# One Mamba-2 layer with MLP and experts: the scan's quadratic part on two halves of 64 tokens instead of one block of 128

## The reference, cut to what matters

```python
dt = softplus(zxbcdt[..., -N_HEADS:] + dt_bias)
decay = exp(dt * -exp(A_log))
def step(h, t):                       # h: (B, 24, 16, 64), one step per token
    dec, dtt, xt, bt, ct = t
    h = dec[..., None, None] * h + (dtt[..., None] * xt)[..., None] * bt[:, None, None, :]
    y = einsum('bhpn,bn->bhp', h, ct)
    return h, y
y = (ys + D * xh) * silu(z)
```

## Time and profile before

| | |
|---|---|
| profiled execution, its own time | 1016.41 us |
| its span | 1014.4 us, mean granted clock 0.962 |
| PE, share of the span | 81% |
| PE weight loads | 63% |
| DVE | 65% |
| ACT | 58% |
| POOL | 34% |

### The profile page before, as it was taken

One profiled execution on the slowest core, in us unless ns is written; L12 is line 12 of the kernel. 1 busy time (PEld: TensorE's weight loads), 2 busy tenths in 40 slices (PEclk: granted clock), 3 DMA queues, 4 the chain that ended last, 5 costly groups with the idle time before them and its releaser, 6 DMA issues.

```text
span 1014.4 us, 22717 instructions
## 1 busy us (share of the span) xinstructions
PE 825.3 (81%) x7120; PEld 637.8 (63%) x7120; DVE 660.8 (65%) x1629; ACT 585.1 (58%) x1307; POOL 345.4 (34%) x508
## 2 busy tenths in 40 slices
PE   3363898888888888888888888888888888888867
PEld 2232676666667666666767666666766666676656
DVE  5565675757667685766768575766768576665524
ACT  3574565665656666665656566565666666565423
POOL 1222333343324344333433334332434433242402
PEclk9675999999999999999999999999999999999988
DMA  8200000000000000000000000000000000000000
GB/s 221 81 1 12 2 6 15 2 20 0 19 0 5 14 0 19 0 19 0 5 14 4 15 0 19 0 20 0 5 14 0 19 0 19 0 5 9 1 8 8
DMA packets 16466, 15.22 MB, mean 15 GB/s; under 512 B 6322, under 2 KB 15224, under 8 KB 16184
## 3 DMA queue, kind: packets, MB, share of 16 engines
q1 hardware_dynamic: 16440, 14.89, 5.5%
HBM read 10.69 MB, written 4.19 MB: 15 GB/s over the span
## 4 chain that ended last, share of the span: by engine, by line
PE 42%; DVE 23%; issue 16%; ACT 13%; POOL 3%; DVEq 1%; ACTq 1%; DMA 0%; POOLq 0%; SPq 0%
PE bank L1305 20%; DVE mr L1024 5%; DVE xa L966 4%; PE bank L1471 4%; PE bank L1513 3%; PE bank L1588 3%; PE bank L1537 3%; DVE w_raw L1188 2%; ACT L687 2%; ACT xk L651 2%; ACT L812 2%; ACT er L706 2%; DVE e_ge L1117 2%; POOL t L476 1%; PE bank L1450 1%
## 5 line engine op out<-in xcount | busy, mean ns | idle before, releaser
L1024 DVE SCALAR_TENSOR_TENSOR mr<-er,gm 128x512 f32<-128x512 f32 x192 | 129.2, 702 | 58.1 <-ACT er L706 57.7
L540 POOL TENSOR_TENSOR w_raw<-w_raw 128x384 f32<-128x384 f32 x96 | 99.2, 1034 | 145.9 <-ACT w_raw L767 143.6
L778 ACT ACTIVATE sg<-bank 128x256 f32<-128x256 f32 x144 | 55.3, 384 | 136.2 <-PE bank L1305 135.9
L1588 PE MATMUL bank<-w2t,w_raw 128*128 128x192 f32 x576 | 116.4, 329 | 7.4 <-ACT w_raw L767 7.4
L706 ACT ACTIVATE er<-bank 128x512 f32<-128x512 f32 x192 | 104.3, 597 | 30.4 <-PE bank L1450 29.9
L1471 PE MATMUL bank<-mr,xd 128*32 128x128 f32 x1536 | 90.9, 288 | 28.0 <-DVE mr L1024 26.6
L966 DVE SCALAR_TENSOR_TENSOR xa<-xr,cw_,xa 128x256 f32<-128x256 f32 x192 | 101.4, 536 | 4.4 <-ACT xa L617 0.4
L1305 PE MATMUL bank<-x_h,w_hi 128*128 128x256 f16 x288 | 79.9, 277 | 29.6 <-DVE w_raw L1188 27.5
L1188 DVE TENSOR_TENSOR w_raw<-sg,bank 128x256 f32<-128x256 f32 x144 | 60.3, 420 | 61.5 <-ACT sg L778 56.3
L1588 PEld LDWEIGHTS bank<-w2t,w_raw 128*128 128x128 f32 x576 | 90.5, 190 | 13.3 <-ACT w_raw L767 9.6
L737 ACT ACTIVATE sg<-bank 128x256 f32<-128x256 f32 x96 | 36.9, 384 | 105.2 <-PE bank L1305 104.8
(11 more groups left out here) (233 smaller groups left out, 2160.4 us busy)
## 6 DMA issues: line engine op xcount, KB each, us to landing
out<-w_raw SPq DMA_DIRECT2D x16, 192.0 KB, 2.0
w_raw<-weights SPq DMA_DIRECT2D x1, 1924.0 KB, 9.6
wt_raw<-weights SPq DMA_DIRECT2D x2, 962.0 KB, 14.9
pos<-position SPq DMA_DIRECT2D x16, 96.0 KB, 2.8
tok<-tokens SPq DMA_DIRECT2D x16, 70.0 KB
sums<-lj SPq DMA_DIRECT2D x16, 64.0 KB, 2.2
ri<-sums SPq DMA_DIRECT2D x64, 12.0 KB
w2t<-w SPq DMA_DIRECT2D x1, 864.0 KB, 19.7
```

Source lines behind the costliest of these rows:

```text
L540: pool.tensor_tensor(acc[:], acc[:], wt_out[:, e % NWT], ALU.add).then_inc(acc_done, 1)
L778: act.activation(sg[:, e % 2, :], p_pair[e % 2][:, 0:NB * Q], ACT.Silu).then_inc(sx_ready, 1)
L1024: ve.scalar_tensor_tensor(mr[:, r % NER], er[:, r % NER], 1.0, gm[:, b, :].unsqueeze(1).to_broadcast([128, HG, Q]), ALU.min, ALU.mult)\
L1588: ins = pe.matmul(p_out[(e + 1) % 2][:, b * D:(b + 1) * D], hh[:, e % NHH, b * Q:(b + 1) * Q], w2t[:, e, :], start=True, stop=True)
```

## The change

A chunk's 128 tokens are taken as two halves of 64 (`QB`). Pairs of tokens within one half go through the exponent, mask and product path; partition j of a tile holds the first half's j in 0..63 and the second half's in 64..127, so one tile of 128 x 512 now covers 8 heads (`HG` = 8, `NQ` = 3, 6 units a chunk). `exponents` for the middle unit of a sequence is two matmuls of 256 columns. The products are done for each half by itself: 64 rows, 64 columns, by `masked_products`; the second group on the same unit waits for the first (`yh_done`).

What the second half takes from the first goes through a middle state: POOL makes `middle` = `state` times the decay over the first half and `xm` = `xd` times the decay from j to the middle (`to_middle`, ahead of `weighted_x` in each scan), and `state_read` becomes nine fp32 matmuls of 64 columns: `state` for the first half, `middle` and `xm` (with `gx`, the C·B products of the second half with the first) for the second. It waits for both POOL results. `ends` doubles to four sets, by six more matmuls in `running_sums`. `masked_g` becomes three operations.

`ri` has 64 instead of 128 columns a head, and is filled by 16 DMAs of two partitions, each row in pieces of 64 fp16 values, instead of 4. `setup_first` on VectorE has nine operations more (masks `ones_first`, `after_first`, zeros), `setup_exponents` half as wide ones.

Orders change too: on TensorE `state_share(f, 0)` and `project_in_x(p)` move ahead of the last products of their scan; on VectorE the state read's scaling (`from_state`), `mixed` and `pre_onehot`, and `norm2_apply` and `steps_dt` come behind the last mask of their scan; on ScalarE `mixed_norm` comes behind the third exponential.

```diff
-HG = 4
+HG = 8
+QB = Q // 2
...
+def unit_parts(q):
+    parts = []
+    for f in range(2):
+        heads = range(max(q * HG, f * HF), min((q + 1) * HG, (f + 1) * HF))
+        if len(heads):
+            parts.append((f, heads[0] - f * HF, heads[0] - q * HG, len(heads)))
+    return parts
...
-        ends = sb("ends", [128, 2, NB, NH])
-        eend, wend = ends[:, 0], ends[:, 1]
+        ends = sb("ends", [128, 4, NB, NH])
+        eend, wend, emid, wmid = (ends[:, k] for k in range(4))
...
-        ri = sb("ri", [128, NB, 2, HF, Q], F16)
-        gm = sb("gm", [128, NB, Q])
+        ri = sb("ri", [128, NB, 2, HF, QB], F16)
+        gd = sb("gd", [128, NB, QB])
+        gx = sb("gx", [128, NB, QB])
...
-        er = sb("er", [128, NER, HG, Q])
-        mr = sb("mr", [128, NER, HG, Q])
...
-                        sp.dma_start(ri[HF:HF + 4, b, f, :, :],
-                                     sums[b, f].rearrange("(g r) i -> g r i", g=4)[:, 0:HF, :]).then_inc(ri_in, 16)
+                        for part in range(2):
+                            for half in range(2):
+                                row = 16 * part + HF + half
+                                sp.dma_start(ri[row:row + 3:2, b, f, :, :],
+                                             sums[b, f].rearrange("(g k r) (s i) -> k s g r i", g=2, k=2, s=2)
+                                             [part, half, :, 0:HF, :]).then_inc(ri_in, 16)
...
+            def scaled_state(b, dst, factor):
+                return pool.tensor_tensor(dst[:, b, :].rearrange("n (h p) -> n h p", h=NH),
+                                          state[:, b, :].rearrange("n (h p) -> n h p", h=NH),
+                                          factor[:, b, :].unsqueeze(2).to_broadcast([128, NH, HD]), ALU.mult)
+            def to_middle(c, b):
+                pool.wait_ge(eend_ready, c + 1)
+                if later(c):
+                    pool.wait_ge(s_ready[b], c)
+                    pool.wait_ge(yi_done[b], c)
+                settle(pool)
+                scaled_state(b, middle, emid).then_inc(s_middle[b], 1)
+                pool.wait_ge(xd_ready[b], c + 1)
+                weighted(c, b, xm, wmid).then_inc(xm_ready[b], 1)
...
+                    to_middle(f, 0)
                     weighted_x(f, 0)
...
             def body(p, f, b):
                 if f is not None:
-                    scan(f, 0, {} if b is None else {2: lambda: mixed(b), 4: lambda: mixed_norm(b)})
+                    scan(f, 0, {} if b is None else {2: lambda: mixed(b)})
+                    if b is not None:
+                        mixed_norm(b)
                 elif b is not None:
                     mixed(b)
...
                 ve.wait_ge(bt_ready, c + 1)
-                ve.tensor_tensor(gm[:], p_y[:, 0:NB * Q].rearrange("p (b i) -> p b i", b=NB),
-                                 upper[:].unsqueeze(1).to_broadcast([128, NB, Q]), ALU.mult).then_inc(gm_ready, 1)
+                if later(c):
+                    ve.wait_ge(yi_done[1], c)
+                g = p_y[:, 0:NB * Q].rearrange("p (b i) -> p b i", b=NB)
+                for half in (slice(0, QB), slice(QB, Q)):
+                    ve.tensor_tensor(gd[half], g[half, :, half], upper[half, half].unsqueeze(1).to_broadcast([QB, NB, QB]),
+                                     ALU.mult)
+                ve.tensor_copy(gx[0:QB], g[0:QB, :, QB:Q]).then_inc(gm_ready, 1)
             def operands(c):
...
                         ve.wait_ge(yq_done, c * NR + r - NER + 1)
                     ve.scalar_tensor_tensor(mr[:, r % NER], er[:, r % NER], 1.0,
-                                            gm[:, b, :].unsqueeze(1).to_broadcast([128, HG, Q]), ALU.min, ALU.mult)\
+                                            gd[:, b, :].unsqueeze(1).to_broadcast([128, HG, QB]), ALU.min, ALU.mult)\
                         .then_inc(m_ready, 1)
                     if q in between:
                         between[q]()
...
+            def from_state(c, b):
+                ve.wait_ge(yi_done[b], c + 1)
+                ve.wait_ge(ecx_ready[0], c + 1)
+                ve.wait_ge(ecx_ready[1], c + 1)
+                if later(c):
+                    ve.wait_ge(y_sum[b], c)
+                ve.tensor_tensor(t1[:, b], p_misc[:, 0:DI].rearrange("p (k i) -> p k i", k=KT), ecx[:, :, b, :],
+                                 ALU.mult).then_inc(t1_ready[b], 1)
             def scanned(c, b):
...
                     mixed(b)
                 if f is not None:
-                    scan(f, 0, {} if b is None else {3: mixed_and_tokens})
+                    scan(f, 0, {})
+                    from_state(f, 0)
+                    if b is not None:
+                        mixed_and_tokens()
                 elif b is not None:
                     mixed(b)
                 if b is not None:
                         setup_first()
                     pre_split(p)
                 if f is not None:
-                    scan(f, 1, {} if b is None else {1: lambda: norm2(b), 3: lambda: norm2_apply(b),
-                                                     4: lambda: None if p is None else steps_dt(p)})
+                    scan(f, 1, {} if b is None else {1: lambda: norm2(b)})
+                    if b is not None:
+                        norm2_apply(b)
+                        if p is not None:
+                            steps_dt(p)
+                    from_state(f, 1)
                 elif b is not None:
                     second_input(b)
...
-                pe.matmul(o, after16[:], pb[:, :, 0:2, 16:16 + HF], start=False, stop=True).then_inc(cum_done, 1)
+                pe.matmul(o, after16[:], pb[:, :, 0:2, 16:16 + HF], start=False, stop=True)
+                for k, of in enumerate((ones_first, after_first), 2):
+                    o = p_misc[:, 256 + k * NB * NH:256 + (k + 1) * NB * NH]
+                    pe.matmul(o, of[:], pa[:, :, 0:2, 0:HF], start=True, stop=False)
+                    pe.matmul(o, of[:], pa[:, :, 0:2, 16:16 + HF], start=False, stop=False)
+                    ins = pe.matmul(o, of[:], pb[:, :, 0:2, 16:16 + HF], start=False, stop=True)
+                ins.then_inc(cum_done, 1)
             def sums_on_channels(c):
...
             def exponents(c, r):
                 b, q = divmod(r, NQ)
-                f = q // (NQ // 2)
                 if r == 0 and not later(c):
                     pe.wait_ge(setup_v, SETUP_V)
                 if r == 0:
-                    pe.wait_ge(ri_in, c * 64 + 64)
+                    pe.wait_ge(ri_in, c * 256 + 256)
                 if r < 2:
                     pe.wait_ge(ecx_ready[r], c + 1)
                 else:
                     pe.wait_ge(e_ready, c * NR + r - 1)
-                heads, step = unit_heads(q)
-                of = slice(heads[0] - f * HF, heads[-1] - f * HF + 1, step)
-                pe.matmul(p_d[r % 2][:].rearrange("p (h i) -> p h i", h=HG), lj[:, b, f, :], ri[:, b, f, of, :],
-                          start=True, stop=True).then_inc(d_done, 1)
-            def scan(c, b, between, p=None):
+                exponent = p_d[r % 2][:].rearrange("p (h i) -> p h i", h=HG)
+                for f, first, at, n in unit_parts(q):
+                    ins = pe.matmul(exponent[:, at:at + n], lj[:, b, f, :], ri[:, b, f, first:first + n, :], start=True, stop=True)
+                ins.then_inc(d_done, 1)
+            def masked_products(c, units, half, place):
+                pe.wait_ge(m_ready, c * NR + units[-1] + 1)
+                if place == 1:
+                    pe.wait_ge(yh_done, c * 4 + (0, 2, 3, 5).index(units[0]) + 1)
+                settle(pe)
+                rows = slice(half * QB, (half + 1) * QB)
+                for r in units:
+                    b, q = divmod(r, NQ)
+                    for odd in range(2):
+                        for j in range(odd, HG, 2):
+                            row, col = j // 2 * 32, q * Q + half * QB
+                            ins = pe.matmul(p_y[row:row + 32, col:col + QB], xd[rows, b, q * HG + j, :],
+                                            mr[rows, r % NER, j, :], start=(odd == 0), stop=(odd == 1))
+                if place == 0:
+                    ins.then_inc(yh_done, 1)
+                else:
+                    ins.then_inc(yq_done, len(units))
+            def scan(c, b, between, last, p=None):
                 if b == 0:
                     pe.wait_ge(eend_ready, c + 1)
                     pe.wait_ge(gm_ready, c + 1)
                     pe.wait_ge(bt_ready, c + 1)
                 else:
                     pe.wait_ge(y_sum[0], c + 1)
...
+                first = b * NQ
+                if b == 0:
+                    exponents(c, first + 2)
+                else:
+                    exponents(c, first + 1)
+                    exponents(c, first + 2)
+                masked_products(c, (first, first + 1), 0, 0)
+                state_read(c, b, p)
+                masked_products(c, (first, first + 1), 1, 1)
```

(61 more changed lines are left out.)

57 lines of the change are left out of this document (35 added, 22 removed).

## The result

The changed kernel takes **1133.97 us** (median of 4 runs, 1133.12 to 1135.49) against 1015.12 (4 runs, 1013.69 to 1015.45): 1.118 times the time before, 95% interval 1.116 to 1.120. The forecast of 1011.6 was wrong, and so was its range. The profiled execution has a span of 1133.7 us (1014.4 before) at a mean granted TensorE clock of 0.891 (0.962 before).

A forecast was written before the change was run, and what follows sets the result against it. Bound: a chain of waits through two scan stages, not TensorE. Fourteen iterations at -0.75 give -10.5, last scan -0.4, start +7.6: -3.3 us, so 1011.6 against 1014.93; own range 1006 to 1017, wider 1002 to 1033.

The forecast's parts named there:

- the price of a row load's issue: Sixteen row loads on SP issue 0.33 us apart; the last lands near 504.6, 0.6 us ahead of need.
- Row loads late: Rival: issues 0.45 apart delay each chunk's first exponent 1.3 us, 1031 us; 0.65 apart, 4 us each, 1072; chance 0.25.
- Rounds of 64 columns at 0.055 us: Product groups in both scans: rounds last 0.055 us, 0.43 per half of a unit pair, so no change in stream.
- rounds not halved: Rival: a product round stays at 0.10 to 0.11 us; first stage +0.8, second +0.3, 15 times: 1027 us; chance 0.12.
- State read 1.93 us: Each scan's state read: eighteen records at 0.107 us, paced by weight loads, 1.93 instead of 0.64 us, +1.3.
- The stream's price: Rival: state read costs only its streamed columns, 0.9 us less in each first scan, 999 us; chance 0.08.
- Second scan -0.85: Second scan stage up to the convolution taps: earlier `xn` and x projection bring taps to 538.4 instead of 539.26.
- First scan -0.1: First scan stage: transposes of `vn` start at 511.85 instead of 511.96 us.
- POOL +0.2: First scan: `to_middle` operations on POOL delay VectorE's second mask, cost 0 to 0.5 us, taken as 0.2.
- SwiGLU stage: The second scan's new POOL pair lies in POOL's idle SwiGLU time, at no cost.
- Start +7.6: Start: setup +1.8, chunks 0 and 1 loads +1.6 each, low-clock state reads +3.6, halved `ri` setup -1; bounds 3 and 11.
- 0.5 to 0.9: Sign: the prediction is wrong if a full iteration is not shorter by 0.5 to 0.9 us.

The follow-up runs named there:

- contiguous_rows: The changed kernel with `sums` laid out in DRAM by half, so four row loads a chunk, each to four neighbouring partitions, replace sixteen; median 1047.07 us.
- before_stepped_row_loads: The kernel before with only its row loads changed to sixteen a chunk, each to two partitions a step of two apart; 1126.26 us, 1.1095.
- no_pool_beside_masks: contiguous_rows plus four useless matmuls in the second scan's gap, first-scan `xw` and second-scan middle state moved later on GpSimd; 1006.8 us, 0.9913.

## Why the prediction was wrong

**The failed step is the price of a row load's issue.** It said "I take 0.33, the row of the same tile". Issues stand 0.64 apart, so the last lands 11.4 us behind the first instead of 6.3, and the first exponent product comes 4.6 us later than before in every chunk, by estimate 16 x 4.6 = 74 of the 119 us. The rival "Row loads late" was the case, at the bound I had named (1072 us with issues 0.65 apart) and had given too little weight; what lies between its 1072 and the measured 1134 is mainly the term below and a longer start. I had a measured upper row, the `sums` store's 0.63, and set it aside for resemblance: same tile, same queue. The reason that I gave for the rival, pieces of 128 bytes, was wrong as well; it is the step between the partitions.

**A term was missing: TensorE's clock.** Of 7.1 us in chunk 8 that rival explains 4.6. The rest comes from stretches at 1.2 GHz, behind the wait (the output projection) and in the second scan: those two parts take 21.4 us, and 18.5 at full clock in `contiguous_rows`. My sum, and the 1072 us of the rival too, took a chunk at full clock for granted, because before it had that nearly throughout (the earlier trace rows have 1.00). The slow stretch behind the wait comes with the late loads: `before_stepped_row_loads` has it without the split. The one in the second scan comes with the split: it is there without late loads in `contiguous_rows`, where it takes 3.9 us whenever it lasts 10.2. That the split takes matmul columns from TensorE is a likely reason, but not one that a run shows.

**The other terms**, read from full-clock stretches of `contiguous_rows`, as here in its first scan:

```profile
467.40 0.65 PE L1529 MATMUL bank<-mr,xd 64*32 64x64 f32 x32 [0.50 <-DVE mr L1075]
467.98 0.43 PE L1576 MATMUL bank<-xs,state 128*128 128x64 f32 x2
468.25 0.39 PE L1578 MATMUL bank<-xs,middle 128*128 128x64 f32 x2
468.47 0.39 PE L1579 MATMUL bank<-gx,xm 128*128 128x64 f32 x2
```

- Rounds of 64 columns at 0.055 us: right; 32 records take 0.65. The rival "rounds not halved" is out.
- State read 1.93 us: right within 0.2; its pairs stand 0.22 apart (467.98 to 470.13 for all 18). The stream's price is out.
- Second scan -0.85: -0.83 to the taps, and by the way forecast. Behind the stage's first exponential the second half of `xn` comes 0.33 us earlier than before (0.3 forecast) and the x projection 1.38 (1.39).
- First scan -0.1 and POOL +0.2: together +0.1 forecast, +0.24 measured. The pair of masks took 1.93 us instead of 1.29 and `xw` 1.37 instead of 0.84, dearer than my bound of 0.5; without it, in `no_pool_beside_masks`, the same part gains 0.32. By the rule that I had weighed (the Trainium skill, "SBUF — State Buffer", "Who interferes with whom") I had worked out up to 0.84 us: the 0.64 is nearer to it than my 0.2.
- SwiGLU stage, forecast 0 since "the new pair lies in POOL's idle SwiGLU time": +0.23. POOL was idle there, but VectorE made `un` beside it, 0.89 us for the second half instead of 0.37. Idle time of one engine was no free place while the other one worked.
- Start +7.6: in `no_pool_beside_masks` chunk 1's first load comes 59.2 us behind chunk 0's instead of 51.6, +7.6. The equal number is luck. That kernel has four row loads a chunk, so my 3.2 for sixteen is not in it, and of the 1.8 for `setup_first` less 1 for `ri` only 0.1 came: chunk 0's loads go out at 40.67 us, 40.58 before. In the changed kernel itself the same interval is 15.7 longer. Much of what came instead is clock (0.59 in that interval, 0.70 before), for which I had only chunk 0's state reads.

So at full clock and with loads in time a chunk is shorter by 0.40 us, where I had said 0.5 to 0.9; with the two orders 1.24.

## What to carry to other kernels

Take the price of a DMA's issue from a row with the same access pattern, the step of its partitions included, or keep the dearest row of that queue as the likely one when a cover is thin; here a layout in DRAM that lets neighbouring partitions be written gave it all back. A change of what TensorE has to do, or a new wait, can cost its clock: read the granted clock of each stretch of both kernels, and compare chunk with chunk at the same clock before judging the rest. Put work on GpSimd where it doesn't slow VectorE down, not just where GpSimd has time, and check that the piece of VectorE's that gets faster is on the chain: the two moves together gave 0.84 us a chunk here, a shorter `un` alone in the kernel before nothing.

## What was not expected of the hardware

- A DMA issue on SP to two partitions a step of two apart took 592 ns; the same bytes to two neighbouring ones 272. 1 piece of 3,072 bytes: 250; 4 rows in 48 pieces of 256 bytes: 308.
- Two chunks whose instructions stood at the same distances up to the fall took 57.5 and 61.4 us. TensorE's clock fell in one of them 1.1 us behind a gap of 1.0 us; the other had the same gap, and there it held.
- In chunk 8 of both kernels with the late loads TensorE was idle for 5.7 us. The granted clock fell to 0.50 in the last part of this wait and came back within the output projection: 1.00 from 567.50 to 571.50, 0.50 from 573 to 575 and 1.00 again from 576 in the changed kernel. The stage behind the wait had 0.81 there and 0.74 in `before_stepped_row_loads`.
- Four useless matmuls a chunk (17.4 us of TensorE's time in all) saved 24 us in one version and 32 in another, by the medians (at least 3.6 and 22, by the nearest runs). What it is exactly that lets the clock fall stays open: filling this gap prevents most of the falls behind it, moving it does not, and in the first chunk five matmuls did not bring the clock back.
